# Conv and attention on 16 images: main products as 32-column tiles, and the orders of attention written anew

## What is computed

```
# layer 0: 32 models of 16 channels, each sees its 3x3 neighbourhood (9*16 = 144 values)
hdn = relu(einsum('bmchw,mdc->bmdhw', per_g, w1) + b1)      # 64 hidden per model
x   = x + einsum('bmdhw,mcd->bmchw', hdn, w2) + b2
# layer 1: non-local attention over the 1024 pixels
theta, phi, g = three projections 512 -> 128, with bias
attn = softmax(theta @ phi, axis=-1)                        # 1024 x 1024 per image
y = attn @ g;   z = (w_w @ y + w_b), batch norm;   out = z + x
```

## Time and profile before

| | |
|---|---|
| median of 3 runs | 1564.57 us |
| the profiled execution | 1565.78 us, span 1564.0 us |
| PE busy | 1502.4 us, 96% |
| DVE, ACT, POOL busy | 58%, 48%, 18% |
| one image in the loop | 94.44 us |
| main products (L424) | 2048 records, 481.5 us of PE busy |

### The profile page before, as it was taken

The page is one execution under the profiler, slowest core; times in us unless marked ns, Lnnn a source line. Parts: engine busy times, 40 slices in busy tenths (PEclk is TensorE's granted clock), DMA queues, the critical chain, the costliest instruction groups (busy, mean ns, idle before and its releaser), DMA issues.

```text
span 1564.0 us, 25314 instructions
## 1 busy us (share of the span) xinstructions
PE 1502.4 (96%) x9348; PEld 823.0 (53%) x9348; DVE 904.8 (58%) x1200; ACT 757.6 (48%) x1205; POOL 285.2 (18%) x134
## 2 busy tenths in 40 slices
PE   7999999999999999999999999999999999999975
PEld 1454655446455454555546555454555546554464
DVE  1374664746547474664846557474574746647464
ACT  2554554555445454554545445554554545545541
POOL 0040310303112040210303113040220403103031
PEclk9999999999999999999999999999999999999997
DMA  8555656646466565645646466464656547456144
GB/s 230 155 198 150 236 165 187 228 144 230 141 212 213 157 219 150 226 164 186 216 141 234 149 208 232 138 231 145 213 188 188 196 143 241 160 187 233 49 152 144
DMA packets 160062, 288.43 MB, mean 184 GB/s; under 512 B 9776, under 2 KB 118320, under 8 KB 160048
## 3 DMA queue, kind: packets, MB, share of 16 engines
q1 hardware_dynamic: 160048, 288.24, 56.8%
HBM read 179.15 MB, written 109.05 MB: 184 GB/s over the span
## 4 chain that ended last, share of the span: by engine, by line
issue 76%; POOL 14%; PE 7%; DVE 2%; POOLq 0%; ACT 0%; DVEq 0%
POOL probs L951 14%; PE ps L424 2%; DVE x_lo L810 1%; PE ps L497 1%; PE ps L498 1%; PE ps L499 1%; DVE probs L801 1%; PE ps L440 1%; PE ps L451 1%; PE ps L467 0%; PE ps L469 0%; PE ps L468 0%; DVE x L828 0%; PE ps L511 0%; PE ps L482 0%
## 5 line engine op out<-in xcount | busy, mean ns | idle before, releaser
L951 POOL TENSOR_TENSOR probs<-probs,row_inv 128x1024 f32<-128x1024 f32 x128 | 284.5, 2233 | 1244.5 <-DVE row_inv L789 1244.5
L424 PE MATMUL ps<-windows,w_main 128*64 128x512 f32 x2048 | 481.5, 604 | 9.1 <-DMA windows<-in_x 8.2
L634 ACT ACTIVATE hidden<-ps,columns 128x512 f32<-128x512 f32 x512 | 317.5, 690 | 241.1 <-PE ps L451 128.7
L424 PEld LDWEIGHTS ps<-windows,w_main 128*64 128x64 f32 x2048 | 130.5, 136 | 306.1 <-issue 195.0
L810 DVE TENSOR_TENSOR x_lo<-x_lo,x_hi 128x1024 fp32r<-128x1024 f32 x128 | 204.6, 1625 | 13.6 <-ACT x_hi L664 13.4
L801 DVE STREAM_TRANSPOSE probs<-probs 128x1024 f32<-128x1024 f32 x128 | 156.3, 1231 | 75.4 <-PE ps L499 63.6
L764 DVE SCALAR_TENSOR_TENSOR x<-ps,columns,windows 128x512 f32<-128x512 f32 x128 | 96.0, 750 | 170.6 <-PE ps L451 151.2
L783 DVE TENSOR_REDUCE neg_max<-ps 128x1 f32<-128x1024 f32 x128 | 153.8, 1211 | 69.8 <-PE ps L484 67.6
L657 ACT ACTIVATE probs<-ps,neg_max 128x1024 f32<-128x1024 f32 x128 | 142.7, 1115 | 94.6 <-DVE neg_max L783 94.6
L497 PE MATMUL ps<-x_hi,arena 128*128 128x256 f32 x512 | 152.1, 297 | 16.8 <-DVE x_lo L810 11.2
L467 PE MATMUL ps<-x_hi,wp_hi 128*128 128x512 f32 x384 | 153.4, 399 | 0.0
(11 more groups left out here) (55 smaller groups left out, 1493.9 us busy)
## 6 DMA issues: line engine op xcount, KB each, us to landing
rows_out<-probs SPq DMA_DIRECT2D x128, 512.0 KB, 2.7
x_lo<-rows_out SPq DMA_DIRECT2D x128, 512.0 KB, 4.8
windows<-in_x SPq DMA_DIRECT2D x112, 562.0 KB, 7.2
out<-x SPq DMA_DIRECT2D x64, 512.0 KB, 3.6
windows<-in_x SPq DMA_DIRECT2D x64, 281.0 KB, 3.8
windows<-in_x SPq DMA_DIRECT2D x32, 280.8 KB, 7.0
rows_out<-g_t SPq DMA_DIRECT2D x16, 512.0 KB, 3.1
x_hi<-rows_out SPq DMA_DIRECT2D x16, 512.0 KB, 5.3
```

What stands on the lines that cost most here:

```text
L424: mm(ps[rows, hidden_bank(s, q), :], w_main[:, p, which, :], shifted(windows[:, w, :], unit // UNITS, half), start=True, stop=False, skip_ ...
L634: activation(hidden[:, s % 2, q, :], ps[:, hidden_bank(s, q), :], ACT.Relu, bias=b1s[:, column:column + 1]).then_inc(hidden_ready, 1)
L951: nc.gpsimd.tensor_tensor(rows, rows, row_inv[:, e].to_broadcast([P, PIXELS]), ALU.mult).then_inc(normalized, 1)
```

## The change

Main products: each 64-column tile becomes two products of 32 columns, with the same moving pixels. Orders: on PE scores 2 and 3 move ahead of the projections of the second half, mains are cut at other places and more of them stand next to dx; ACT, DVE and SP get matching orders. Nothing else is changed: the semaphores and their conditions, the buffers and the arithmetic of each product stay. The core of the diff:

```diff
-                    rows = slice(HIDDEN * which, HIDDEN * (which + 1))
-                    mm(ps[rows, hidden_bank(s, q), :], w_main[:, p, which, :],
-                       shifted(windows[:, w, :], unit // UNITS, half), start=True, stop=False, skip_group_check=True)
+                    for part in range(HIDDEN // UNIT):
+                        columns_of = slice(UNIT * part, UNIT * (part + 1))
+                        rows = slice(HIDDEN * which + UNIT * part, HIDDEN * which + UNIT * (part + 1))
+                        mm(ps[rows, hidden_bank(s, q), :], w_main[:, p, which, columns_of],
+                           shifted(windows[:, w, :], unit // UNITS, half), start=True, stop=False,
+                           skip_group_check=True)
```

More of the change, by code:

```diff
@@ L327, in batch @@
                 send_row(n, 1)
+                send_row(n, 2)
+                fetch_row(n, 0)
                 send_g(n)
-                fetch_row(n, 0)
                 fetch_row(n, 1)
+                fetch_row(n, 2)
+                send_row(n, 3)
                 fetch_g(n)
-                send_row(n, 3)
-                send_row(n, 2)
-                fetch_row(n, 2)
                 fetch_row(n, 3)
@@ L540, in batch @@
                 scores(n, 1)
+                scores(n, 2)
+                scores(n, 3)
                 project(n, 1, TH)
-                scores(n, 2)
                 project(n, 1, G)
-                scores(n, 3)
                 scores(n, 4)
@@ L547, in batch @@
                 if has_next:
-                    mains(n + 1, 0, range(0, 4))
-                    hidden_left(n + 1, 0)
+                    mains(n + 1, 0, range(0, 2))
                 scores(n, 6)
                 if has_next:
-                    mains(n + 1, 1, range(0, 1))
+                    mains(n + 1, 0, range(2, 4))
+                    hidden_left(n + 1, 0)
                 scores(n, 7)
+                if has_next:
+                    mains(n + 1, 1, range(0, 4))
+                    mains(n + 1, 2, range(0, 1))
+                    hidden_left(n + 1, 1)
                 attend(n, 0, has_next)
                 if has_next:
-                    mains(n + 1, 1, range(1, 4))
+                    mains(n + 1, 2, range(1, 4))
                 output(n, 0, 0)
+                if has_next:
+                    hidden_left(n + 1, 2)
                 output(n, 0, 1)
-                if has_next:
-                    hidden_left(n + 1, 1)
-                    mains(n + 1, 2, range(0, 4))
                 attend(n, 1, has_next)
@@ L564, in batch @@
                     dx(n + 1, 0)
-                    hidden_left(n + 1, 2)
+                    mains(n + 1, 3, range(0, 1))
                 output(n, 1, 0)
@@ L568, in batch @@
                 if has_next:
-                    mains(n + 1, 3, range(0, 4))
+                    mains(n + 1, 3, range(1, 4))
                     mains(n + 1, 4, range(0, 1))
@@ L578, in batch @@
                     mains(n + 1, 4, range(1, 4))
-                    mains(n + 1, 5, range(0, 1))
                     hidden_left(n + 1, 4)
-                output(n, 2, 1)
                 attend(n, 3, has_next)
                 if has_next:
-                    mains(n + 1, 5, range(1, 4))
+                    mains(n + 1, 5, range(0, 4))
                     hidden_left(n + 1, 5)
@@ L592, in batch @@
                     dx(n + 1, 4)
-                    mains(n + 1, 7, range(0, 4))
+                    mains(n + 1, 7, range(0, 3))
                     dx(n + 1, 5)
+                    mains(n + 1, 7, range(3, 4))
                     hidden_left(n + 1, 7)
@@ L700, in batch @@
                     relus(n + 1, 0, range(2, 4))
[L701 to L702 removed]
+                round_row(n, 2)
+                if has_next:
+                    relus(n + 1, 1, range(0, 3))
                 round_y(n, 0)
[L704 removed]
+                if has_next:
+                    relus(n + 1, 1, range(3, 4))
                 round_row(n, 3)
+                round_y(n, 1)
                 if has_next:
[L707 to L708 removed]
+                    relus(n + 1, 2, range(0, 4))
                 round_row(n, 4)
[L710 to L711 removed]
                 round_row(n, 5)
[L713 to L714 removed]
                 round_y(n, 2)
[L716 to L718 removed]
                 round_row(n, 6)
                 if has_next:
[L721 removed]
+                    relus(n + 1, 3, range(0, 2))
                 round_row(n, 7)
                 if has_next:
[L724 to L726 removed]
+                    relus(n + 1, 3, range(2, 4))
+                    relus(n + 1, 4, range(0, 3))
                 round_y(n, 3)
                 if has_next:
+                    relus(n + 1, 4, range(3, 4))
+                    round_x1(n + 1, 0)
+                    relus(n + 1, 5, range(0, 3))
+                    round_x1(n + 1, 1)
+                    relus(n + 1, 5, range(3, 4))
+                    relus(n + 1, 6, range(0, 3))
                     round_x1(n + 1, 2)
[L730 removed]
+                    relus(n + 1, 6, range(3, 4))
                     round_x1(n + 1, 3)
[L732 removed]
                     round_x1(n + 1, 4)
@@ L837, in batch @@
                 sum_x1(n, 7)
+                split_x1(n, 7)
                 split_projection(n, 0, TH)
-                split_x1(n, 7)
                 split_projection(n, 0, PH)
@@ L844, in batch @@
                 invert_sum(n, 0)
+                find_max(n, 2)
                 invert_sum(n, 1)
                 transpose_row(n, 0)
-                find_max(n, 2)
+                invert_sum(n, 2)
+                find_max(n, 3)
                 transpose_row(n, 1)
                 split_projection(n, 1, TH)
+                invert_sum(n, 3)
+                transpose_row(n, 2)
+                find_max(n, 4)
                 transpose_g(n)
[L851 to L854, removed]
                 find_max(n, 5)
-                transpose_row(n, 2)
                 transpose_row(n, 3)
+                find_max(n, 6)
+                split_row(n, 0)
+                find_max(n, 7)
                 invert_sum(n, 4)
-                split_row(n, 0)
                 split_row(n, 1)
@@ L862, in batch @@
                 split_g(n)
-                find_max(n, 6)
-                find_max(n, 7)
+                invert_sum(n, 6)
+                split_row(n, 2)
                 transpose_row(n, 4)
@@ L867, in batch @@
                 transpose_row(n, 5)
+                split_row(n, 3)
                 add_out(n, 0, 0)
-                invert_sum(n, 6)
-                split_row(n, 2)
-                split_row(n, 3)
                 invert_sum(n, 7)
@@ L891, in batch @@
                 if has_next:
-                    split_x1(n + 1, 1)
+                    split_x1(n + 1, 0)
+                add_out(n, 2, 1)
+                split_y(n, 3)
+                if has_next:
                     sum_x1(n + 1, 2)
-                split_y(n, 3)
-                add_out(n, 2, 1)
                 add_out(n, 3, 0)
@@ L899, in batch @@
                     sum_x1(n + 1, 3)
+                    split_x1(n + 1, 1)
+                    sum_x1(n + 1, 4)
+                    sum_x1(n + 1, 5)
                     split_x1(n + 1, 2)
-                    sum_x1(n + 1, 4)
                     split_x1(n + 1, 3)
-                    sum_x1(n + 1, 5)
                     split_x1(n + 1, 4)
```

15 lines of the change are left out of this document (8 added, 7 removed).

## The result

Median of four runs 1576.31 us (1575.33 to 1582.17) against 1564.56 for the kernel before beside it: the ratio is 1.0083, 95% interval 1.0064 to 1.0102. The forecast was 1550, range 1543 to 1561. The profiled execution took 1575.33, span 1573.5.

The account below looks back on a forecast made before the run. PE, busy for 96% of the span, was taken as the bound, with group prices and stalls to save: 15 loop images at -1.0 (-15.0), first image -1.0, last +1.6, sum -14.4, giving 1550 us, range 1543 to 1561.

Parts of the forecast that it names:

- Part 1, the tiles: Mains as 32-column tiles: a pair stays 0.86, group prices fall where D and M touch; net -0.5 us per image.
- stall of 0.2: Mains 6, behind dx 3, wait for relu(5,0): 0.2 us with entry, and the same at mains 7.
- Part 2, the walk: New orders walked through one loop image: stalls 2.0 us instead of 2.48, -0.45; the walk ends at 93.4.
- Scores 2: Scores 2, now behind scores 1, wait for exponential 0: a stall of 1.36 + 0.11 us.
- mains due: Main 3 of slot 1 waits for exponential 7, ending 761.85, so a stall of only 0.05 us.
- g's chain: g transposed, sent (3.1) and fetched (5.3), landed 761.0, then rounded and split; attend 0 stalls 0.1 us.
- rival 2: g chain or exponential 7 later than added up: 0.5 to 0.7 late makes 1557 to 1560; chance 0.15.
- Rival 1: POOL keeps its turn over waiting split_g: attend 0 1.9 late instead of 0.1, +27, 1577; chance 0.13.
- Its sign: For POOL keeping the turn: split_g's record is over 3 us and ends past 42.
- The part ahead of it: First image, outside the loop: M beside D seven times, each meeting saves 0.14, together -1.0 us.
- The last image: No mains cover g's chain: attend 0 at 1520.5 instead of 1516.30, attend 1 1.6 later; +1.6, bounds 0 and 4.2.

Follow-up runs that it names:

- e2: The kernel after with the old 64-column product for the mains, so the new orders alone: 1587.28 us (1.0141).
- e5: The kernel after with fetch 2 moved behind the fetch of g and inv 5 moved behind split_g: 1546.79 us (0.9888).
- e3: The kernel after with one DMA moved on SP, fetch 2 behind the fetch of g: 1552.82 us (0.9922).
- e4: The kernel after with the inversion of sum 5 behind split_g on DVE, so normalize 5 can't be issued first: 1569.29 us (1.0031).
- e7: The kernel after with only send 3 moved ahead of fetch 2, which stays ahead of the fetch of g: 1566.93 us over twelve runs (1.0004).
- e1: The orders of the kernel before with mains as four 32-column tiles, so the tiles alone: 1557.86 us (0.9956).
- e6: e5 with PE, DVE and ACT reordered to remove the stall at scores 2, and fetch 1 ahead of the send of g: 1583.73 us (1.0119).
- e9: e8 with exponential 7 and all four relus of slot 0 ahead of round_row 1 on ACT: 1532.10 us (0.9795).
- e8: e6 with every send ahead of fetch 1, transposes 2 and 3 ahead of maximum 5, round_row 0 ahead of exponential 5: 1542.87 us (0.9855).

## Why the prediction was wrong

**Part 1, the tiles: right.** PE's busy time in an image falls by 0.53 from the kernel before to the kernel after, where 0.5 net was worked out. In the new orders the tiles alone bring 0.72 (93.07 in e2's window, 92.35 in the kernel after), where the expectation of e2 had 0.95 less 0.24. A pair is still 0.86, and mains 6 start 0.89 behind dx 3, as the end of an image shows beside the earlier trace rows:

```profile
905.32 1.07 PE L455 MATMUL ps<-hidden,w2s 128*32 128x512 f32 x8
906.21 3.84 PE L427 MATMUL ps<-windows,w_main 128*32 128x512 f32 x32
909.98 1.11 PE L444 MATMUL ps<-windows,w_left 32*64 32x512 f32 x16
```

Twice the records cost nothing. From the start of the mains to the next group are 3.77: 3.57 of mains (four pairs and the group price) plus the stall of 0.2 that was forecast for relu(5,0).

**Part 2, the walk: right for the engines, wrong for the transfers.** Scores 2 at 16.32, 1.59 behind the record ahead instead of the usual 0.23, maximum 7 ending at 36.73, mains due at 37.9, mains 6 and 7 late by 0.2: each came within 0.1 us. e5 shows the sum of it, 93.4.

**The step that failed** is the one on g's chain: "SP sends it (3.1 to landing) and fetches it (5.3), landed 761.0; SP has send 2, fetch 0, fetch 1, fetch 2, send 3 around them, all issued by 755." It takes medians from the order before, where only the end of send 1 was in flight ahead of the send of g, and fetches 0 and 1 ahead of its fetch; in the new order it is fetch 0 ahead of the send, and fetches 1, 2 and send 3 ahead of the fetch. And it treats being issued as the end of what the others cost. In the run the send took 3.95 and the fetch 6.7, and g landed at 39.3 into the image instead of 37.0. The same step hid a wait that I had not listed (rival 2 names exponential 7 as late, without a reason): it may not start before send 3 has left its row buffer. In the old order send 3 stood ahead of fetch 2. Behind fetches 1 and 2 it took 7.05, and so exponential 7 came at 38.0 instead of 36.7. That is the 1.1 at the mains of slot 1 in this image, 1.3 in the mean. e3 takes one fetch out of its way and gets 36.76.

**What made 0.7 into 1.9.** Rival 2 named the late chain and priced it at 1557 to 1560, for 0.5 to 0.7 late. Two things were missing in it. First the size: by e4, with the turn out of the way, exponential 7 alone puts attend 0 at 41.8 to 43.0, 0.9 to 2.1 late, and g alone would put it 0.3 before that. Second the turn: a late split_g finds normalize 5 already issued and comes out 1.08 behind it, at 42.60, whether it was issued 0.01 or 0.76 behind. That is why 13 of 15 attends start within 0.04 of 42.84 and why images are of two lengths in e3 and e7.

**Rival 1** had nearly the right number (1577), by luck, for a mechanism that isn't there. It let POOL keep the turn over a *waiting* split_g. Its sign, a split_g that ends past 42, came true, but the record was 2.2 long and not over 3. In e3 and e7 every split_g issued ahead of normalize 5, while normalize 4 still ran, got the turn, the latest by 0.06; every one issued behind lost it, the nearest by 0.01, and so did all thirty of the kernel after and e2. This agrees with the sentence of the Trainium skill that was cited for it (SBUF — State Buffer, Summary: rules for kernel authors): the one issued first goes. My application assumed that split_g would be 0.7 ahead; it was 0.76 behind.

**Around the loop.** The part ahead of it gave 2.6 instead of 1.0. The window 21.20 to 24.40 is a clock effect: granted 1.00 here, 0.50 in the kernel before, 1.6 us. In e1, e2, e6 and e9 it was 0.50, in the others 1.00. e6 and e9 have the new tiles and orders too, so it follows neither, and what decides it stays open. The tiles alone fit the forecast: where that window had 0.50, the loop starts at 62.8 and 62.9 with the old tiles and at 61.6 to 62.1 with the new. The last image was forecast at +1.6 and came at -1.2. Attend 0 there starts 41.67 in, 0.7 later than walked, and attend 1 comes 2.9 later than before instead of 1.6. But from the start of attend 3 to the end it takes 11.2 where it took 14.4: the attend itself is 3.10 long instead of 4.61, the mean clock of the image being 0.89 instead of 0.84, and the output behind it waits 0.46 instead of 1.80. The clock and the waits behind attend 0 were taken as fixed.

Against the forecast for the profiled execution, 1551.4: the loop is +28.3, the part ahead -1.6, the last image -2.8, together +23.9, the measured 1575.3. e5, with the walk of the loop come true (1401.2 where 1401.6 was forecast), is at 1545.2 by the same parts: 2.2 less ahead of the loop, and 3.6 less in the last image.

## What to carry to other kernels

When an order of DMA issues changes, walk the queue as you walk an engine: here each transfer of the chain landed behind those issued before it, so a median from another order is no duration, and a send whose buffer someone waits for goes ahead of fetches that have room. For each instruction moved, list all its waits from the code, the release of the buffer it writes included, even if the trace of before shows none of them as binding. Where two engines take turns, a delay of 0.03 us can cost a whole turn (1.85 here): leave such a race some margin, or take it out through the other's inputs, as e4 does.

## What the runs showed of the hardware

- The 512 KB sends and fetches that SP issues between scores and attend 0 land in the order of issue, 1.3 to 2.1 us apart in the image shown. Behind two fetches a send takes 7.05, where the sends of e8 take 3.1 to 4.4.
- DVE's two-input split and POOL's normalize run one after the other, by time of issue: 0.06 ahead wins, 0.01 behind loses, and the price is 1.85 (an end at 42.60 instead of 40.75). The loser's record holds its wait (1.7 to 3.0 long instead of 1.23).
- The same idle stretch of PE, 1.86 us ahead of attend 0, was followed by a lower granted clock (0.62 over attend 0, 1.5 us more) in both slow images of e3, and by none in four images of e7 (nor in the fifth, with 1.68). In e6 it fell in ten of fifteen images, behind 2.3 us of idle PE that all fifteen had. No run told why.
